# A macaron block in fp32: layer norms by four lanes of 32 columns on TensorE, and gate halves ahead of up halves

## What is computed

```python
x = x + 0.5 * ffn(layernorm(x), gate_W, gate_s, up_W, up_s, down_W, down_s)
x = x + attn(layernorm(x), w_qkv, b_qkv, w_out, b_out)      # 16 heads of 32, causal
x = x + 0.5 * ffn(layernorm(x), ...)                        # the same weights again

def layernorm(x, eps=1e-5):
    return (x - mean(x)) / sqrt(var(x) + eps)               # over the 512 features
def ffn(x):                                                 # weights are 4-bit codes with scales
    gate = x @ Wg.T; up = x @ Wu.T                          # 512 -> 4096
    return (gelu_tanh(gate) * up) @ Wd.T                    # 4096 -> 512
```

## Time and profile before

| | |
|---|---|
| median of three runs | 3046.81 us |
| profiled execution, its own time | 3048.34 us |
| its span (first to last instruction) | 3046.5 us |
| mean granted TensorE clock, as a share of 2.4 GHz | 0.985 |
| TensorE matmul busy | 2947.0 us (97%) |
| VectorE / ScalarE / GpSimd busy | 1881.9 / 1060.0 / 760.9 us |

### The profile page before, as it was taken

How to read it: one execution, slowest core, us unless ns; L and a number is a source line. 1 busy time by engine, 2 the same in 40 slices (tenths; PEclk the granted TensorE clock), 3 DMA queues, 4 the chain that set the end, 5 groups by cost and what they waited for, 6 DMA issues and landing times. The chain is left out here.

```text
span 3046.5 us, 38836 instructions
## 1 busy us (share of the span) xinstructions
PE 2947.0 (97%) x13152; PEld 2208.8 (73%) x13152; DVE 1881.9 (62%) x3314; ACT 1060.0 (35%) x1797; POOL 760.9 (25%) x481
## 2 busy tenths in 40 slices
PE   6999999999999979999999999789999999999999
PEld 3788888888888857754454554468888888888887
DVE  7666565566565555566666665776556656556654
ACT  3322222222222222265565665242222222222222
POOL 4422222222222234400000002343222222222221
PEclk8999999999999999999999999899999999999999
DMA  3000000000000016822322332100000000000001
GB/s 97 21 28 25 24 28 21 21 28 24 24 28 21 1 45 127 220 54 50 63 54 50 61 82 65 48 19 30 21 21 28 21 28 28 21 21 28 21 14 56
DMA packets 120234, 126.75 MB, mean 42 GB/s; under 512 B 72728, under 2 KB 72984, under 8 KB 116820
## 3 DMA queue, kind: packets, MB, share of 16 engines
q1 hardware_dynamic: 120148, 125.71, 15.8%
HBM read 96.34 MB, written 29.34 MB: 41 GB/s over the span
## 5 line engine op out<-in xcount | busy, mean ns | idle before, releaser
L61 PE MATMUL psum<-ffn_x_high,ffn_w_high 128*128 128x512 f32 x2048 | 803.9, 393 | 20.7 <-POOL ffn_x_low L174 17.5
L62 PE MATMUL psum<-ffn_x_low,ffn_w_high 128*128 128x512 f32 x2048 | 800.2, 391 | 0.0
L63 PE MATMUL psum<-ffn_x_high,ffn_w_low 128*128 128x512 f32 x2048 | 799.9, 391 | 0.0
L536 POOL TENSOR_TENSOR ffn_inner<-ffn_gelu,ffn_inner 128x512 fp32r<-128x512 f32 x256 | 346.7, 1354 | 1159.2 <-ACT ffn_inner L480 1159.2
L385 DVE SCALAR_TENSOR_TENSOR ffn_gelu<-ffn_gelu,psum 128x512 f32<-128x512 f32 x256 | 176.0, 688 | 596.6 <-ACT ffn_gelu L473 596.6
L61 PEld LDWEIGHTS psum<-ffn_x_high,ffn_w_high 128*128 128x128 f32 x2048 | 386.3, 189 | 113.3 <-issue 19.6
L63 PEld LDWEIGHTS psum<-ffn_x_high,ffn_w_low 128*128 128x128 f32 x2048 | 386.4, 189 | 80.8
L62 PEld LDWEIGHTS psum<-ffn_x_low,ffn_w_high 128*128 128x128 f32 x2048 | 386.7, 189 | 80.4 <-issue 1.0
L61 PE MATMUL psum<-ffn_inner,ffn_w_high 128*128 128x512 f32 x1024 | 398.6, 389 | 0.2
L63 PE MATMUL psum<-ffn_inner,ffn_w_low 128*128 128x512 f32 x1024 | 398.4, 389 | 0.0
L62 PE MATMUL psum<-ffn_inner,ffn_w_high 128*128 128x512 f32 x1024 | 398.3, 389 | 0.0
(11 more groups left out here) (116 smaller groups left out, 3066.0 us busy)
## 6 DMA issues: line engine op xcount, KB each, us to landing
ffn_words<-packed SPq DMA_DIRECT2D x96, 256.0 KB
ffn_word_scales<-scales SPq DMA_DIRECT2D x96, 256.0 KB
qk_parts<-parts SPq DMA_DIRECT2D x32, 512.0 KB, 4.2
queries<-qk_parts SPq DMA_DIRECT2D x48, 256.0 KB, 4.0
keys<-qk_parts SPq DMA_DIRECT2D x48, 256.0 KB, 6.1
x<-x_in SPq DMA_DIRECT2D x4, 1024.0 KB, 14.5
v_parts<-parts SPq DMA_DIRECT2D x16, 256.0 KB, 4.7
values<-v_parts SPq DMA_DIRECT2D x16, 256.0 KB, 7.9
```

The lines of the kernel that those rows point to most:

```text
L61: pe.matmul(out, w_high, x_high, start=first, stop=False, skip_group_check=True)
L62: pe.matmul(out, w_high, x_low, start=False, stop=False, skip_group_check=True)
L63: return pe.matmul(out, w_low, x_high, start=False, stop=last, skip_group_check=True)
L536: pool.tensor_tensor(inner[:, tb % 2, m, 1, :], product[m], f32(inner[:, tb % 2, m, 0, :]), ALU.subtract)\
```

## The change

The layer norm is made otherwise, and the queues of all engines are written anew for it.

- The sums use a stationary matrix of 128 rows by 32 columns. The 512 tokens are four quarters of 128 columns, and quarter j goes to output partitions 32j to 32j+31 (`quarter_sums`): 16 matmuls of 32x128 for the four feature tiles. `sum_pairs` and `sum_square_pairs` are gone; TensorE reads `x` and `squares` itself.
- The result, 128x128, holds a token's mean in one lane only. ScalarE copies it to SBUF (`take_mean`), and four matmuls of 128x128 by 128 columns with one-hot rows (`spreaders`) spread it over all partitions (`spread_mean`).
- Sqrt and reciprocal work on 128x128, then four matmuls spread the inverse into the variance bank (`spread_inverse`), from which `scale` reads it.
- Constants are made once for the three norms (`NormConstants`).
- `gate_up_tile` becomes two calls of `gate_up_part`, and at the start of a feed-forward the gate halves of both tiles of block 0 stand ahead of their up halves. VectorE unpacks UP later, and GpSimd splits it after the first block's `low`.

```diff
-    def sum_pairs(self, engine, tb):
-        ...
-    def mean(self, pe, tb):
-        ...
+    def quarter_sums(self, pe, bank, tile, k):
+        for j in range(QUARTERS):
+            last = pe.matmul(bank[quarter(j), 0:P], self.averager[:], tile[:, cols(j, P)],
+                             start=(k == 0), stop=(k == KT - 1), skip_group_check=True)
+        return last
+
+    def spread(self, pe, bank, quarters):
+        for j in range(QUARTERS):
+            last = pe.matmul(bank[:, cols(j, P)], self.spreaders[:, j, :], quarters[:], start=True, stop=True,
+                             skip_group_check=True)
+        return last
+
+    def sums(self, pe, tb):
+        if self.x_loaded is not None:
+            pe.wait_ge(self.x_loaded[tb], 16)
         if tb >= 2:
             pe.wait_ge(self.centred_ready, tb - 1)
+        for k in range(KT):
+            last = self.quarter_sums(pe, self.mean_bank[tb % 2], self.x[:, k, cols(tb, TB)], k)
+        last.then_inc(self.sums_ready, 1)
+
+    def take_mean(self, act, tb):
+        act.wait_ge(self.sums_ready, tb + 1)
+        if tb >= 1:
+            act.wait_ge(self.mean_ready, tb)
+        act.activation(self.mean[:], self.mean_bank[tb % 2][:, 0:P], ACT.Copy).then_inc(self.mean_taken, 1)
+
+    def spread_mean(self, pe, tb):
+        pe.wait_ge(self.mean_taken, tb + 1)
+        self.spread(pe, self.mean_bank[tb % 2], self.mean).then_inc(self.mean_ready, 1)
...
-    def sum_square_pairs(self, dve, tb):
-        ...
     def variance(self, pe, tb):
-        pe.wait_ge(self.square_pairs_ready, tb + 1)
         if tb >= 2:
-            pe.wait_ge(self.std_ready, tb - 1)
-        for k in range(2):
-            last = pe.matmul(self.var_bank[tb % 2], self.averager[:], self.squares[:, k, :],
-                             start=(k == 0), stop=(k == 1))
+            pe.wait_ge(self.normed_ready, KT * (tb - 1))
+        for k in range(KT):
+            pe.wait_ge(self.squares_ready, KT * tb + k + 1)
+            last = self.quarter_sums(pe, self.var_bank[tb % 2], self.squares[:, k, :], k)
         last.then_inc(self.variance_ready, 1)
...
-        act.activation(self.std[:], self.var_bank[tb % 2], ACT.Sqrt, bias=self.eps[:]).then_inc(self.std_ready, 1)
+        act.activation(self.std[:], self.var_bank[tb % 2][:, 0:P], ACT.Sqrt, bias=self.eps[:])\
+           .then_inc(self.std_ready, 1)
...
+    def spread_inverse(self, pe, tb):
+        pe.wait_ge(self.rstd_ready, tb + 1)
+        self.spread(pe, self.var_bank[tb % 2], self.std).then_inc(self.spread_ready, 1)
...
-            dve.tensor_tensor(tile, tile, self.std[:], ALU.mult).then_inc(self.normed_ready, 1)
+            dve.tensor_tensor(tile, tile, self.var_bank[tb % 2], ALU.mult).then_inc(self.normed_ready, 1)
```

More of the change, by code:

```diff
@@ L63, in split_products, with quarter, __init__, fill @@
     return pe.matmul(out, w_low, x_high, start=False, stop=last, skip_group_check=True)
+QUARTERS = TB // P
+def quarter(j):
+    return slice(j * HD, (j + 1) * HD)
+class NormConstants:
+    def __init__(self, nc, ctx):
+        self.averager = ctx.enter_context(nc.sbuf_tensor("averager", [P, HD], F32))
+        self.eps = ctx.enter_context(nc.sbuf_tensor("eps", [P, 1], F32))
+        self.spreaders = ctx.enter_context(nc.sbuf_tensor("spreaders", [P, QUARTERS, P], F32))
+        self.mean = ctx.enter_context(nc.sbuf_tensor("mean", [P, P], F32))
+        self.std = ctx.enter_context(nc.sbuf_tensor("std", [P, P], F32))
+        self.ready = ctx.enter_context(nc.semaphore("constants_ready"))
+    def fill(self, dve):
+        dve.memset(self.averager[:], 1.0 / D).then_inc(self.ready, 1)
+        dve.memset(self.eps[:], EPS).then_inc(self.ready, 1)
+        dve.memset(self.spreaders[:], 0.0).then_inc(self.ready, 1)
+        dve.wait_ge(self.ready, 3)
+        for j in range(QUARTERS):
+            dve.memset(self.spreaders[j * HD:j * HD + 1, j, :], 1.0).then_inc(self.ready, 1)
+    def wait(self, engine):
+        engine.wait_ge(self.ready, 3 + QUARTERS)
 class Norm:
-    def __init__(self, nc, ctx, tag, x, x_high, x_low, centred, squares, pairs, std, averager, eps,
-                 mean_bank, var_bank, x_loaded):
+    def __init__(self, nc, ctx, tag, x, x_high, x_low, centred, squares, constants, mean_bank, var_bank, x_loaded):
         def sem(name):
@@ L224, in ffn @@
         n = Norm(nc, ctx, tag, x, x_high, x_low, [centred0[:, :, :], centred1[:, :, :]],
-                 squares[:, :, :], pairs[:, :, :], std, averager, eps,
-                 down_bank[0:2], down_bank[2:4], x_loaded)
+                 squares[:, :, :], constants, down_bank[0:2], down_bank[2:4], x_loaded)
         words_loaded = [sem(f"words_loaded{p}") for p in range(NPIECE)]
@@ L414, in group @@
                     add_down(gg, s, tb)
-            dve.memset(averager[:], 1.0 / D).then_inc(n.constants_ready, 1)
-            dve.memset(eps[:], EPS).then_inc(n.constants_ready, 1)
-            n.sum_pairs(dve, 0)
+            if x_in is not None:
+                constants.fill(dve)
             n.centre(dve, 0)
             unpack(0, 0, GATE, first=True)
-            n.sum_square_pairs(dve, 0)
-            unpack(0, 0, UP, first=True)
             n.invert(dve, 0)
@@ L489, in group @@
                         weight_high(gg + s, 1 - s, tb)
-            act.wait_ge(n.constants_ready, 2)
+            if x_in is not None:
+                constants.wait(act)
+            n.take_mean(act, 0)
             n.square(act, 0)
+            n.standard_deviation(act, 0)
             weight_high(0, 0, GATE)
-            n.standard_deviation(act, 0)
-            weight_high(0, 0, UP)
+            n.take_mean(act, 1)
             n.high(act, 0)
@@ L841, in project_in @@
         n = Norm(nc, ctx, "qkv", x, x_high, x_low, [heads.norm_centred[:, tb, :, :] for tb in range(2)],
-                 squares, heads.norm_pairs[:], std, averager, eps, bank[4:6], bank[6:8], None)
+                 squares, constants, bank[4:6], bank[6:8], None)
         wv_loaded = sem("wv_loaded")
```

234 lines of the change are left out of this document (120 added, 114 removed).

## The result

The changed kernel took 3017.23 us (median of 4 runs, 3016.56 to 3018.48) beside 3048.36 us for the kernel before (3045.04 to 3049.94): ratio 0.9898, 95% interval 0.9886 to 0.991, that is -31.1 us. Forecast were 3020 us and -28.5.

A forecast was written before the change was run, and what follows sets the result against it. Latency chains of the layer norms at three starts were taken to bound the kernel, TensorE otherwise being busy. Savings of 8.0, 10.9 and 9.6 us sum to -28.5 against 3048.34, so 3020 us, range 3009 to 3043.

The forecast's parts named there:

- What bounds the kernel: TensorE is 97% busy; its four longest waits, 59.2 us, lie in the layer norms starting the three parts.
- A group of sums at 1.3 us: 16 quarter matmuls on TensorE: 1.0 us plus 0.3 for going to lanes and back, 2.6 at half clock.
- A spread at 0.95: Four 128x128 matmuls by 128 columns on TensorE: 0.95 us at full clock, 1.9 at half.
- `scale` from PSUM: VectorE's scale takes the same time from PSUM as from SBUF and no longer stretches while GpSimd works.
- First products: The starts' first products come at 27.2, 1122.3 and 1962.5 us, for 33.76, 1133.49 and 1971.78.
- The new wait for block 1's mean: First feed-forward: block 1's mean copy stands ahead of block 0's high parts; its sums start only at 22.2 us.
- From the first product to the end of the start: Products, sums, spreads and remaining waits: 55.2 us in the first feed-forward, ending at 82.4 for 90.40.
- block 2's tile at half clock: First feed-forward: 4.3 us of waits for the tile behind block 2's low parts, paced by GpSimd.
- 2.1 for block 2's low parts: First feed-forward: 2.1 us of wait, as these low parts stand behind a gelu tile on ScalarE and GpSimd.
- UP weights just in time: First feed-forward: UP weights split by 37.7 us, first product due at 39.1; if later, the next wait.
- Rival "the lanes don't overlap": Lanes run one after the other, 3.7 us a group; decides from about 2.5; +65 us, 3085, chance 0.08.
- Rival "the clock stays low": TensorE stays at 1.2 GHz through each start up to its first tile: 3032 us, chance 0.13.

The follow-up runs named there:

- e6: The changed kernel with every group of 16 quarter matmuls done twice: 3032.68 us.
- e8: The changed kernel with block 1's sums where TensorE idles, its x loaded earlier, ScalarE's table loaded by a dummy copy, two similar moves in the projections: 3014.16 us.
- e1: The changed kernel with the UP half of tile (0, 0) back directly behind block 1's variance, nothing else moved: 3039.47 us.
- e3: The changed kernel with each group's 16 quarter matmuls ordered lane by lane, the variance waiting for all four squares: 3048.92 us.
- e5: The changed kernel with the old order of halves, UP unpacked ahead of block 0's inverse, first gelu tile ahead of block 1's high parts: 3027.81 us.
- e7: The changed kernel with the saved 384 columns of reciprocal given back on VectorE for all blocks: 3039.82 us.
- e10: A 3009.93 us version of the changed kernel (earlier sums, block 3's centre later), plus quarter matmuls into an unused bank where TensorE idles: 3013.8 us.

## Why the prediction was right, by its own steps

- **What bounds the kernel**, the three starts: right. All of the -31.2 but 1.9 lies in them or in the pair sums at their heads: -8.2, -9.9 and -11.3, for a forecast of -8.0, -9.6 and -10.9.
- **A group of sums at 1.3 us**, 1.0 and 0.3 for going to lanes and back: 1.01 from its start to the next one's, and 1.94 at half clock for 2.6. Four lanes overlap fully: in e6 a pass of 32 records takes 0.87. Not all of the switch is in the 1.01. The step from the last product to a group is 0.32 us (35.29 to 35.61) and from the first product behind a group to the next 0.35 (32.62 to 32.97), for 0.23 between products. With these a group costs TensorE 1.2 us, 0.87 and some 0.35 for the switch, so both terms were nearly right. The Trainium skill ("TensorE: Matmul & The Clock Gate", Part 3) has three column tiles at 2.38 times the speed of one, 0.79 of ideal. By an estimate from that, the records alone would take 1.08 us; the trace doesn't agree, and the measured 0.87 decides.
- **A spread at 0.95**: 1.00 from the start of one to the next matmul (36.62 to 37.62), 2.0 at half clock for 1.9. No load shows. Reciprocal 0.95 for 0.88, Sqrt 0.37 for 0.36, the mean's copy 0.28 for 0.3.
- **`scale` from PSUM** never stretches: right, 0.68 to 0.69 in all 48, also beside GpSimd (out of SBUF, before, it was 1.79 at worst). What that alone is worth no run tests:

```profile
L203 DVE TENSOR_TENSOR ffn_centred<-ffn_centred,psum x32: 679/681/690, 22.7 to 1997.1; 128x512 f32<-128x512 f32 x32
L203 DVE TENSOR_TENSOR qkv_centred<-qkv_centred,psum x16: 679/682/690, 1110.9 to 1151.6; 128x512 f32<-128x512 f32 x16
```

- **First products** at 27.2, 1122.3 and 1962.5, which are 20.6, 16.5 and 17.0 us behind the norms' starts that the prediction took. Measured is 26.90, and the three lie 19.3, 16.7 and 17.0 us behind their first sums. The first and the third number are luck in part. In the first, x came 1.0 us later than taken (7.59 for 6.6), and two groups at half clock took 1.94 for 2.6 and made good for it. In the third, the first spread ran at half clock (1.99 for 0.95), and the group ahead of the products took 1.94 for 2.6. In the projections the value weights, worked out from 248 GB/s to land 4.5 us behind the norm's start, landed 4.9 behind the first sums (1102.48), and the chain behind them held.
- **The new wait for block 1's mean** is there, and e8 took it away.
- **From the first product to the end of the start**, 55.2 and 55.6, in the projections 52.1: 55.3, 55.3 and 51.7. Inside it terms erred against each other, and that the sum came out to 0.1 us is luck. Too large: 4.3 us for block 2's tile at half clock, which was 1.8 at full clock, and 6.5 for five groups, which were 5.0 from their starts to what follows. Not in the sum: a second wait for a gelu tile, 1.2 us at 75.13, and some 3 us in small pieces, since a run of products takes 0.1 to 0.3 us more than 0.227 us a product where it begins behind a group, a spread or a wait (the 12 from 32.62 take 2.99, for 2.72). Right: 2.1 for block 2's low parts (2.09), 1.2 for the first gelu's product (1.36). For the second feed-forward the prediction adds 11.65 of waits where the first had 11.2, and gives no reason for the difference.
- **UP weights just in time**: 37.2 for the forecast 37.7, due at 38.4. What they cost when that cover is gone was said in one sentence and put at no price; e1 measured 9.9 and 10.7 us in the two feed-forwards.
- **Rival "the lanes don't overlap"**: e3 made half of it true and gave its break-even. **Rival "the clock stays low"**: up to the first product it did in the feed-forwards (granted 0.60 from 1925 to 1942, for 0.72 from 1945 to 1971 before), much of which the forecast had priced at half clock; from there on the reverse, 0.94 for 0.86 in the second feed-forward.
- **Where the 2.6 us beyond the forecast came from**: 0.8 are the three starts together, and 1.9 the attention, chance of the clock as far as I can tell. From the value items to the second norm the profiles without pair sums have 759.0 to 763.5 us for the same code. What decides on which side one falls is open, and no run tested it.

What the prediction didn't know, and what it didn't need, is how the 31 us hang together. It priced the parts one by one along one schedule, and the order of events in that schedule was right; but the parts aren't terms of a sum. Undone alone, the order costs 22 (e1) or 10 (e5), the short reciprocal 23 (e7), the lanes' order 32 (e3), together far over 31.

## What to carry to other kernels

Draw the queue of each engine up to the first product and work out the schedule as a whole; the gain of an edit is what the schedule with it ends at, not its own saving, and here an order worth nothing was worth 4 us in one feed-forward once the pair sums were gone, and 8 in the two with the new norm. Where a step moves onto an in-order engine that bounds the kernel (here the spread of the inverse), everything that feeds it must be short or early, for the later blocks too: in each feed-forward the wide reciprocal cost the three later blocks about twice what it cost the first. When an operand is "just in time", write down what stands behind its wait on all the engines: a late one of 4.5 us cost 10.

## What the runs showed of the hardware that I had not expected

- Lanes of 32 columns in plain fp32 overlap fully in rotation: 32 records of 128 columns in 0.87 us, for 3.5 one by one. The 3.5 is an estimate from 0.109 us a record. In lane-by-lane order the group takes 2.39, so part of the overlap is left even then.
- Going to lanes and back costs about 0.35 us a group: 0.14 inside it (1.01 less 0.87), 0.09 ahead of it and 0.12 behind its first product. A spread, which uses the whole array, has 0.08 of this behind it too (0.31 from 59.40 to 59.71, for 0.23).
- One integer step on VectorE, 0.43 us alone, took 2.45 beside GpSimd (e5), while the product with an operand in PSUM kept its 0.68.
- TensorE idle for 2 us fell to half clock in one kernel and not in another, at the same place in the attention (the two windows above, 0.60 and 1.00). More work ahead kept it up in e6, but work added for that alone (e10) raised it in one place and gained no time.
